# A mixture-of-experts stage on one core: router by pairwise maxima, half lists joined by a flip, the last shared block moved behind the experts

## The chip, the cores and the metric

The kernel runs on one core of a Trainium2 chip. Its time is the device time of one execution in microseconds (us), and a comparison uses the median of several runs. The engines are TensorE (PE; PEld is its weight load), VectorE (DVE), ScalarE (ACT), GpSimd (POOL) and SyncE (SP), which here only starts transfers. The transfers run on 16 DMA engines. Transfers that SyncE starts are on the hardware queue q1, those that GpSimd starts (gathers, scatter-adds, accumulating copies) on the software queue q0.

## What is computed

Four residual layers on x of 2048 tokens (4 x 512) and 512 features: an expert layer routed by token id, an MX-quantised feed-forward layer, cross attention, and last a mixture of 64 experts with a shared expert. Only the last is touched by the change:

```python
scores = sigmoid(x @ gate_w)                 # 2048 x 64
scores_b = scores + bias
gs = scores_b.reshape(-1, 8, 8)              # 8 groups of 8 experts
group_scores = sum(top_k(gs, 2)[0], -1)      # the two largest of each group
keep the 4 best groups, then the 6 best experts among them
w = scores of the six / their sum * 2.5
for each expert: its first 96 tokens (CAP = 96)
    h = silu(x @ w_gate) * (x @ w_up);  y += w * (h @ w_down)      # F = 192
shared = (silu(x @ ws_gate) * (x @ ws_up)) @ ws_down               # F = 192
x = x + tanh(g_ffn[1]) * (y + shared)
```

## The kernel before

Everything is fp32 in this stage. P = 128, D = 512, T = 2048 tokens = 16 tiles (NT), GCH = 4 blocks of 512 tokens, F1 = 192 = 128 + 64 (FR = 64 is the remainder).

The stage is one block of code (from line 1320) in which each engine has its own list of instructions in a fixed order. Semaphores connect them: `need(engine, sem, n)` waits until sem has counted n, and `own.link(...)` makes the next instruction of the same engine wait for this one.

- VectorE normalises the 16 tiles into xnb (line 1424). TensorE turns each (`turn_four`, 1551) through PSUM banks 0 and 1 in turn, and ScalarE copies the columns to XNT (1691). Two `logits` products (1561), each of two blocks, are copied out, turned back (1569) and put through Sigmoid (1700).
- `route(h)` on VectorE (1433 to 1481) treats tiles 0 to 7 (h = 0) and 8 to 15 (h = 1). It finds the two largest of each group by reductions and an equality mask (1438 to 1450), the four best groups by MAX8 and MATCH_REPLACE8 (1453, 1456), masks the others (1458 to 1465), finds the six best experts (1468, 1471), and writes a mask (1473), a key for each chosen token and expert (1476), and the weights selw (1477 to 1481).
- TensorE turns the keys (`turn_keys`, 1607), so that partition e + 64 h holds expert e's keys of token half h. ScalarE copies them (1731). VectorE's `largest` takes the 96 largest of 1024 keys, eight at a time: 12 MAX8 (1491), 11 MATCH_REPLACE8 (1493). TensorE moves the two half lists side by side (`turn_halves`, 1614), VectorE copies them (1498), takes the 96 largest of the 192, TensorE turns the result (`turn_lists`, 1619), and five VectorE instructions (1503 to 1508) make the row indices idx.
- The shared expert goes in four blocks of 512 tokens. `shared_up(g)` (364) does gate and up: a part of 128 features (m = 0) and a part of 64 (m = 1). ScalarE takes Silu and a copy (1716 to 1720), GpSimd multiplies (1366), `shared_down(g)` (1599) makes four tiles in banks 4 and 5, each by a product over 128 rows and one over 64. ScalarE scales and copies (1727), GpSimd adds into X (1370), and SyncE stores the tile to out (1333). TensorE's order is: up 0, up 1, down 0, keys, up 2, down 1, up 3, half lists, down 2, two tiles of down 3, lists, two tiles of down 3.
- SyncE loads the weights of the 32 expert pairs into 7 places (`load_pair`, 374 and 376). Pairs 0 and 1 are there long before. Pairs 2, 4 and 3 take the places of X tiles and of XNT when these have been read and stored.
- GpSimd gathers rows of 96 tokens per expert (1383). In the loop over pairs, TensorE turns rows (1639), multiplies gate and up (1648), turns the hidden (1656), and multiplies down (1667) as pairs of 64-row halves. VectorE copies the result (1528), and GpSimd scatter-adds it (1390): even experts into out, odd experts into odd_sum. At the end one accumulating transfer of 4 MB adds odd_sum to out (1413).

## Time and profile before

| | |
|---|---|
| runs, median (lowest to highest) | 1090.39 us (1089.48 to 1091.29), 3 runs |
| profiled execution: its time, its span | 1089.95 us, 1087.9 us |
| mean granted TensorE clock | 0.962 |
| busy: PE, DVE, POOL, ACT | 90%, 62%, 59%, 37% |

The span is the time from the first to the last instruction in the profile; 2.05 us lie around it. The busy share of TensorE is a mean over stages with different limits. In the part that the change touches, from about 640 us on, it is 1.00 through most of the expert loop and 0 in the last 28 us.

### The profile page before, as it was taken

The numbers are of one execution on the slowest core, as the hardware profiler recorded it, in microseconds if no ns is written. First come the engines' busy times: TensorE is split into PE (matmuls) and PEld (weight loads), VectorE is DVE, ScalarE is ACT, GpSimd is POOL, SyncE is SP. The second block draws the span as 40 slices with busy tenths as digits, with TensorE's granted clock in tenths as the row PEclk, the third lists the DMA queues.
The fourth block names the chain that finished last, engine by engine and source line by source line (L and its number), as shares of the span: only waits on it lengthen the run. The fifth ranks groups of instructions, "written<-read, shape, count | busy, mean of one in ns | idle before, by whom it ended". The sixth has DMA issues, their size and how long they took to land. (4 is left out here: it accounts for less than half of the span.)

```text
span 1087.9 us, 13655 instructions
## 1 busy us (share of the span) xinstructions
PE 975.8 (90%) x4400; PEld 473.8 (44%) x4400; DVE 673.8 (62%) x1244; ACT 400.9 (37%) x797; POOL 643.6 (59%) x564
## 2 busy tenths in 40 slices
PE   5989999479999998999999988997999999999960
PEld 4445544234444443444444443333555555555520
DVE  6689988968888887677777758891222222222220
ACT  4345444334444444666666633322111111111100
POOL 4487885668787887776776721345355555454530
PEclk9989999789999999999999999998999999999995
DMA  7664454420000001501006040148999999999547
GB/s 262 229 146 113 131 134 99 103 82 1 1 1 1 1 2 39 193 20 30 20 20 237 1 154 1 58 162 283 349 340 343 342 340 345 345 338 340 126 57 154
DMA packets 63124, 161.72 MB, mean 149 GB/s; under 512 B 9824, under 2 KB 9968, under 8 KB 62480
## 3 DMA queue, kind: packets, MB, share of 16 engines
q1 hardware_dynamic: 46880, 115.76, 30.2%
q0 software_dynamic: 16048, 40.91, 17.1%
q10 hardware_dynamic: 128, 4.19, 1.1%
q8 instruction: 37, 0.61, 0.2%
q14 instruction: 31, 0.25, 0.1%
HBM read 129.54 MB, written 39.67 MB: 156 GB/s over the span
## 5 line engine op out<-in xcount | busy, mean ns | idle before, releaser
L578 POOL TENSOR_TENSOR ARENA<-ARENA 128x512 f32<-128x512 f32 x128 | 133.2, 1062 | 54.2 <-DVE ARENA L821 54.2
L1390 POOL DMA_INDIRECT out<-ARENA,idx x32 | 46.2, 1445 | 131.7 <-DVE ARENA L1528 124.2
L1004 PE MATMUL PS<-SLAB,ARENA 128*128 128x512 bf16 x512 | 118.0, 382 | 6.7 <-DVE ARENA L772 4.6
L1755 ACT ACTIVATE ARENA<-PS 96x192 f32<-96x192 f32 x64 | 20.9, 326 | 227.5 <-PE PS L1648 227.5
L1528 DVE COPY ARENA<-PS 96x512 f32<-96x512 f32 x64 | 41.1, 682 | 93.9 <-PE PS L1667 93.9
L1225 ACT ACTIVATE ARENA<-PS,ARENA 128x512 f32<-128x512 f32 x128 | 86.8, 683 | 23.6 <-DVE ARENA L815 20.3
L815 DVE TENSOR_REDUCE ARENA<-PS 128x2 f32<-128x1024 f32 x64 | 78.2, 1222 | 6.9 <-PE PS L1038 6.5
L1648 PE MATMUL PS<-SLAB,ARENA 128*96 128x384 f32 x240 | 82.1, 495 | 0.0
L1004 PEld LDWEIGHTS PS<-SLAB,ARENA 128*128 128x128 bf16 x512 | 48.8, 98 | 67.8 <-issue 13.2
L1049 PEld LDWEIGHTS PS<-ident,ARENA 128*128 128x128 f32 x512 | 54.8, 141 | 51.1 <-issue 35.0
L1191 ACT ACTIVATE ARENA<-PS 128x512 f32<-128x512 f32 x64 | 38.2, 597 | 102.9 <-PE PS L1004 84.3
L534 POOL TENSOR_TENSOR ARENA<-ARENA 128x1024 bf16<-128x1024 fp8e4 x32 | 61.1, 1909 | 24.8 <-DVE ARENA L786 24.8
L528 POOL TENSOR_TENSOR ARENA<-ARENA 128x1024 f32<-128x1024 f32 x32 | 62.8, 1962 | 20.0 <-DVE ARENA L781 20.0
L958 PE MATMUL PS<-CT,XNT 128*128 x152 | 71.6, 615 | 2.2 <-ACT XNT L1129 2.1
L1038 PE MATMUL PS<-ARENA 64*128 64x512 f32 x256 | 73.2, 649 | 0.3 <-ACT ARENA L1225 0.2
L942 PE MATMUL PS<-CT,ARENA 128*128 x152 | 70.7, 609 | 2.9 <-ACT ARENA L1119 2.9
L1049 PE MATMUL PS<-ident,ARENA 128*128 128x128 f32 x512 | 70.7, 280 | 1.7 <-DVE XNT L828 1.7
L1516 DVE SCALAR_TENSOR_TENSOR ARENA<-PS,ARENA 96x192 f32<-96x192 f32 x64 | 26.2, 409 | 73.9 <-ACT ARENA L1755 73.9
L1383 POOL DMA_INDIRECT ARENA<-rows,idx x64 | 60.0, 937 | 19.7 <-issue 11.1
L1061 PE MATMUL PS<-XNT,CT 128*64 128x512 f32 x256 | 68.2, 616 | 0.0
L471 POOL TENSOR_TENSOR XNT<-XNT,ARENA 128x1536 f32<-128x1536 f32 x16 | 45.6, 2850 | 35.1 <-DVE ARENA L675 35.0
L1023 PE MATMUL PS<-SLAB,ARENA 128*128 128x512 bf16 x256 | 58.6, 380 | 0.0
(254 smaller groups left out, 1879.1 us busy)
## 6 DMA issues: line engine op xcount, KB each, us to landing
SLAB<-in_L_ffn_w_gate SPq DMA_DIRECT2D x30, 384.0 KB, 19.8
SLAB<-in_L_ffn_w_up SPq DMA_DIRECT2D x30, 384.0 KB, 20.8
X<-in_L_ffn_w_down SPq DMA_DIRECT2D x14, 768.0 KB, 18.5
SLAB<-in_L_ffn_w_down SPq DMA_DIRECT2D x10, 768.0 KB, 18.5
CT<-in_L_ffn_w_gate SPq DMA_DIRECT2D x16, 384.0 KB, 19.7
CT<-in_L_ffn_w_up SPq DMA_DIRECT2D x16, 384.0 KB, 21.0
X<-in_ctx SPq DMA_DIRECT2D x4, 1024.0 KB, 8.8
XNT<-in_L_ffn_w_gate SPq DMA_DIRECT2D x16, 256.0 KB, 2.6
```

The costliest lines, as they stand in the source:

```text
L528: pool.tensor_tensor(blocks(iy[:, h, :]), blocks(inter[:, par, h, :]), spread(iinv[:, h, :]), ALU.mult).then_inc(iy_ready, 1)
L534: pool.tensor_tensor(blocks(qi[:, par, h, :]), blocks(ic[:, h, :]), spread(im[:, par, h, :]), ALU.mult).then_inc(iq_ready, 1)
L578: last = pool.tensor_tensor(prob[s % 4][:, h, :], prob[s % 4][:, h, :], rec[:, s % 4, h:h + 1].to_broadcast([P, D]), ALU.mult)
L815: dve.tensor_reduce(nmax[:, s % 4, :], bank(2 * (s % 2), 2).rearrange("p (h d) -> p h d", h=2), AX.X, ALU.max, negate=True).then_inc(max_r ...
L942: last = pe.matmul(bank(2 + j % 2), hT[:, j % 2, k * P:(k + 1) * P], CT[:, bass.ds(e, 1), k, :].rearrange("p a s -> p (a s)"), start=(k == ...
L958: last = pe.matmul(bank(4 + j % 2), aT[:, j % 2, k * P:(k + 1) * P], CT[:, bass.ds(e, 1), k, :].rearrange("p a s -> p (a s)"), start=(k == ...
L1004: last = pe.matmul(bank(b), QT[:, par, k * P:(k + 1) * P], w[:, k, c * D:(c + 1) * D], start=(k == 0), stop=(k == KD - 1))
L1038: last = pe.matmul(bank(2 * (s % 2) + h), qn[rows_h, i % 2, c * P:(c + 1) * P], keys4[rows_h, i % 4, :], start=True, stop=True)
L1049: last = pe.transpose(bank(4 + h)[:, k * P:(k + 1) * P], prob[s % 4][:, h, k * P:(k + 1) * P], ident[:, :])
L1061: last = pe.matmul(bank(6 + i % 2)[h * DH:h * DH + DH, :], CT[:, b, k, r * P + h * DH:r * P + h * DH + DH], PT[h][i % 2][:, k, :], start=( ...
L1225: last = act.activation(prob[s % 4][:, h, :], bank(2 * (s % 2) + h), ACT.Exp, bias=nmax[:, s % 4, h:h + 1], accum_out=esum[:, s % 4, h:h + 1])
L1648: last = pe.matmul(bank(2 + e % 2)[0:CAP, 0:2 * F1].rearrange("p (n f) -> p n f", n=2), bT[:, e % 2, k, :], gate_up_of(e)[:, :, k, :], sta ...
```

## The change

Six things change, and nothing outside this stage.

1. The two largest of each group are found by pairwise `max` and `min` over neighbours: 64 columns to 32, 16 and 8 per tile, 10 two-input operations in place of three reductions, two masks and five narrow steps. Masking the groups is one operation that adds -1e30. The mask and the key product are one operation. The weights of both halves follow both passes.
2. ScalarE runs one Sigmoid on a dummy value ahead of the stage. Tiles are turned through four banks (0, 1, 4, 5), and a third group of four is turned ahead of the first logits.
3. The half lists are sorted, with zeros behind the last token. The second one is turned around by a product with a flip matrix and fills the empty end of the first, so the search over 192 and the last turn go.
4. The shared expert's down product takes two tiles at a time: the two products over 128 rows, then the remainders of 64 rows, one on partitions 0 to 63 and one on 64 to 127. ScalarE writes the remainders of every second tile to the other partitions, in four half copies.
5. TensorE's order is: up (0,0), (0,1), (1,1), keys, up (1,0), down 0, up 2, down 1, half lists, two tiles of down 2, flip, two tiles of down 2.
6. Block 3 of the shared expert moves behind the expert loop. Its raw X tiles 12 to 15 are stored to out early. Its products run after the last expert, and four accumulating transfers of 128 rows add them to out. The merge is split: rows of tiles 12 to 15 (1 MB) first, then the other 3 MB. The four transfers are issued once the first part has landed, on the same queue.

The diff, cut to its core:

```diff
+        NS = NT - KD
+        ORDER = [(0, 1), (1, 0), (0, 1), (0, 1)]
+
+        def up_count(g, m):
+
+            return 2 * g + ORDER[g].index(m) + 1
+
+        TURN = (0, 1, 4, 5)
+
+        def rest_of(a):
+
+            return a[:, D:SW].rearrange("p (q c) -> p q c", q=2)
+
+        def tiles_of(a, odd):
+
+            return a.rearrange("p (q two c) -> p q two c", q=2, two=2)[:, :, odd, :]
...
+                for i in range(NS, NT):
+                    sp.dma_start(out_v[:, i, :], X[:, i, :]).then_inc(acc_stored[2], 16)
...
                         sp.wait_ge(acc_stored[0], 64)
                         load_pair(sp, 2)
                     if i == 8:
-                        sp.wait_ge(sgu_done, 2 * GCH)
+                        sp.wait_ge(sgu_done, 2 * (GCH - 1))
                         load_pair(sp, 4)
-                    if i == 12:
+                    if i == NS - 1:
...
+                own.link(pool.memset(flip, 0.0))
+                pool.affine_select(out=flip, in_=flip, compare_op=ALU.not_equal, fill=1.0, base=1 - CAP,
+                                   pattern=[[1, CAP]], channel_multiplier=1).then_inc(iota2_set, 1)
...
-                pool.dma_start(out[0:T, :], odd_sum[0:T, :], accum_op=ALU.add, max_dma_last_dim=4 * 4 * D).then_inc(merged, 16)
+                pool.dma_start(out[NS * P:T, :], odd_sum[NS * P:T, :], accum_op=ALU.add, max_dma_last_dim=4 * 4 * D).then_inc(merged_l, 16)
+                pool.dma_start(out[0:NS * P, :], odd_sum[0:NS * P, :], accum_op=ALU.add, max_dma_last_dim=4 * 4 * D).then_inc(merged, 16)
+                pool.wait_ge(merged_l, 16)
+                for n in range(KD):
+                    pool.wait_ge(sh_ready, NS + n + 1)
+                    pool.dma_start(out_v[:, NS + n, :], sh_l[:, n, :], accum_op=ALU.add).then_inc(shared_added, 16)
...
+                    one_of, other = halves(sc_b[:, tiles].rearrange("p i e -> p (i e)"))
+                    dve.tensor_tensor(high, one_of, other, ALU.max)
+                    own.link(dve.tensor_tensor(low, one_of, other, ALU.min))
+                    dve.tensor_tensor(first4, *halves(high), ALU.max)
+                    dve.tensor_tensor(less4, *halves(high), ALU.min)
+                    own.link(dve.tensor_tensor(next4, *halves(low), ALU.max))
+                    own.link(dve.tensor_tensor(next4, next4, less4, ALU.max))
+                    dve.tensor_tensor(first8, *halves(first4), ALU.max)
+                    dve.tensor_tensor(less8, *halves(first4), ALU.min)
+                    own.link(dve.tensor_tensor(next8, *halves(next4), ALU.max))
+                    own.link(dve.tensor_tensor(next8, next8, less8, ALU.max))
...
+                    own.link(dve.tensor_scalar(gsm[:, 4, tiles], gext[:, tiles, 0:GROUPS], -BIG / 2, -BIG, ALU.is_gt, ALU.mult))
+                    own.link(dve.tensor_tensor(grouped(ext[:, tiles, 0:E1]), grouped(sc_b[:, tiles]),
+                                               gsm[:, 4, tiles].unsqueeze(3).to_broadcast([P, count, GROUPS, PERG]), ALU.add))
...
+                    dve.scalar_tensor_tensor(out=keyt[:, h], in0=ext[:, tiles, 0:E1], scalar=-1.5 * BIG, in1=spread(keyc[:, tiles], E1),
+                                             op0=ALU.is_le, op1=ALU.mult).then_inc(key_ready, 1)
+
+                def weights(h):
+
+                    tiles = slice(NT // 2 * h, NT // 2 * (h + 1))
+                    own.link(dve.scalar_tensor_tensor(out=selw[:, tiles], in0=ext[:, tiles, 0:E1], scalar=-1.5 * BIG, in1=scores_sb[:, tiles],
+                                                      op0=ALU.is_le, op1=ALU.mult))
...
                 route(0)
                 route(1)
+                weights(0)
+                weights(1)
...
+                for n in range(CAP // 8):
+                    eight = half_lists[:, 8 * n:8 * n + 8]
+                    if n == CAP // 8 - 1:
+                        dve.max(eight, keys).then_inc(list_ready, 1)
+                    else:
+                        own.link(dve.max(eight, keys))
+                        own.link(dve.match_replace(keys, eight, keys, 0.0))
+
                 dve.wait_ge(list_turned, 1)
+                dve.tensor_copy(both, bank(7)[0:CAP, 0:2 * E1].rearrange("p (h e) -> p h e", h=2)).then_inc(list_ready, 1)
+                dve.wait_ge(list_ready, 2)
                 dve.wait_ge(list_turned, 2)
+                own.link(dve.scalar_tensor_tensor(out=list_c, in0=both[:, 0, :], scalar=0.0, in1=bank(7)[0:CAP, 2 * E1:3 * E1],
+                                                  op0=ALU.is_equal, op1=ALU.mult))
+                own.link(dve.tensor_tensor(list_c, list_c, both[:, 0, :], ALU.add))
+                dve.tensor_scalar(emp[:, 0, :], list_c, 0.0, None, ALU.is_equal)
+                own.link(dve.tensor_scalar(emp[:, 1, :], list_c, -1.0, float(T), ALU.mult, ALU.add))
+                own.link(dve.scalar_tensor_tensor(out=emp[:, 0, :], in0=emp[:, 0, :], scalar=rowf[0:CAP, 0:1],
+                                                  in1=emp[:, 1, :], op0=ALU.mult, op1=ALU.add))
+                dve.tensor_copy(idx[0:CAP, :], emp[:, 0, :]).then_inc(idx_ready, 1)
...
+                dve.wait_ge(ssil_ready, up_count(GCH - 1, 0))
+                dve.tensor_tensor(hs_l[:, 0:D], ssil_l[:, 0:D], bank(1), ALU.mult).then_inc(hs_ready, 1)
+                dve.wait_ge(ssil_ready, up_count(GCH - 1, 1))
+                dve.wait_ge(ub_ready, 2 * GCH - 1)
+                dve.tensor_tensor(hs_l[:, D:SW], ssil_l[:, D:SW], ub_l, ALU.mult).then_inc(hs_ready, 1)
...
+                def shared_down(g, two, into, product):
+
                     pe.wait_ge(hs_ready, 2 * g + 2)
+                    for n in range(2):
+                        pe.matmul(bank(into[n]), product[:, (2 * two + n) * P:(2 * two + n + 1) * P], wsd[:, 0, :], start=True, stop=False)
+                    for n in range(2):
+                        rows_n = slice(n * FR, (n + 1) * FR)
+                        pe.matmul(bank(into[n]), rest_of(product)[rows_n, two, :], wsd[rows_n, 1, :],
+                                  start=False, stop=True).then_inc(sd_done, 1)
+
+                def shared_two(g, two):
+                    need(pe, sh_ready, 4 * g + 2 * two - 2)
+                    if g == 0:
+                        pe.wait_ge(key_out, 2)
+                    shared_down(g, two, ((4, 5), (2, 3))[two], hs[g % 2])
...
+                    pe.transpose(bank(7)[0:CAP, 0:2 * E1], half_lists, ident[:, :]).then_inc(list_turned, 1)
+
+                def turn_around():
                     pe.wait_ge(list_ready, 2)
+                    pe.matmul(bank(7)[0:CAP, 2 * E1:3 * E1], flip[0:CAP, :], both[:, 1, :], start=True, stop=True).then_inc(list_turned, 1)
+
+                pe.wait_ge(sw_in, 80)
+                shared_up(0, 0)
+                shared_up(0, 1)
+                shared_up(1, 1)
                 turn_keys()
+                shared_up(1, 0)
+                for two in range(2):
+                    shared_two(0, two)
+                shared_up(2, 0)
+                shared_up(2, 1)
+                for two in range(2):
+                    shared_two(1, two)
                 turn_halves()
+                shared_two(2, 0)
+                pe.wait_ge(iota2_set, 2)
+                turn_around()
+                shared_two(2, 1)
...
+                pe.wait_ge(bt_out, E1)
+                shared_up(GCH - 1, 0)
+                pe.wait_ge(ht6_out, PAIRS)
+                shared_up(GCH - 1, 1)
+                pe.wait_ge(h6_ready, E1)
+                shared_down(GCH - 1, 0, (2, 3), hs_l)
+                pe.wait_ge(o_ready, E1)
+                shared_down(GCH - 1, 1, (4, 5), hs_l)
...
+                act.activation(rsum[:, 0:1], neg_half[:, 0:1], ACT.Sigmoid)
...
                 columns_out(1)
+                columns_out(2)
                 logits_out(0)
-                columns_out(2)
+                columns_out(3)
                 scores_out(0)
-                columns_out(3)
                 logits_out(1)
                 scores_out(1)
...
+                        for odd in range(2):
+                            last = act.activation(rest_of(ssil)[odd * FR:(odd + 1) * FR], tiles_of(bank(6)[0:FR, :], odd), ACT.Silu)
+                        last.then_inc(ssil_ready, 1)
+                        for odd in range(2):
+                            last = act.activation(rest_of(ub)[odd * FR:(odd + 1) * FR], tiles_of(bank(6)[FR:2 * FR, :], odd), ACT.Copy)
+                        last.then_inc(ub_ready, 1)
...
+                shared_hidden(0, 0)
+                shared_hidden(0, 1)
+                shared_hidden(1, 1)
                 for r in range(4):
                     act.wait_ge(xn_stored[r], XN0 + 16 * NT // 8)
                 keys_out(0)
                 keys_out(1)
+                shared_hidden(1, 0)
+                shared_out(0)
+                shared_hidden(2, 0)
+                shared_hidden(2, 1)
                 shared_out(1)
...
+                act.wait_ge(h6_ready, E1)
+                act.wait_ge(sgu_done, up_count(GCH - 1, 0))
+                act.activation(ssil_l[:, 0:D], bank(0), ACT.Silu).then_inc(ssil_ready, 1)
+                act.wait_ge(sgu_done, up_count(GCH - 1, 1))
+                for odd in range(2):
+                    last = act.activation(rest_of(ssil_l)[odd * FR:(odd + 1) * FR], tiles_of(bank(6)[0:FR, :], odd), ACT.Silu)
+                last.then_inc(ssil_ready, 1)
+                for odd in range(2):
+                    last = act.activation(ub_l.rearrange("p (q c) -> p q c", q=2)[odd * FR:(odd + 1) * FR],
+                                          tiles_of(bank(6)[FR:2 * FR, :], odd), ACT.Copy)
+                last.then_inc(ub_ready, 1)
+                for n in range(KD):
+                    act.wait_ge(sd_done, NS + n + 1)
+                    act.activation(sh_l[:, n, :], bank((2, 3, 4, 5)[n]), ACT.Copy, scale=tgate[:, 3:4]).then_inc(sh_ready, 1)
```

## Rows read from the trace of the kernel before

**Rows 1.** Chain that ended last: start us, length us, engine, output, line, instructions.

```profile
664.74 21.10 PE PS L364 x64
685.84 8.43 PE PS L1599 x16
...
696.10 1.24 DVE CT L1491
697.36 1.30 DVE ARENA L1493 x2
...
726.41 12.65 PE PS L1599 x24
...
741.77 1.10 POOL ARENA L1383
...
743.17 7.37 DMA ARENA<-rows,idx
...
751.50 3.65 PE PS L1648 x8
...
755.60 2.58 PE PS L1648 x8
...
765.06 2.75 PE PS L1667 x12
...
774.41 2.75 PE PS L1667 x12
...
1055.94 4.12 DMA odd_sum<-ARENA,idx
```

**Rows 2.** Waits of SyncE's queue, 740:1060 us: total us, times, longest us.

```profile
SPq L376 <- PE PS L1667: 68.9, 25, 6.1
```

**Rows 3.** Timeline of the tail: start us, us, engine, line, operation [idle before].

```profile
1052.68 1.29 DVE L1528 COPY ARENA<-PS 96x512 f32<-96x512 f32 x2 [2.92 <-PE PS L1667]
...
1061.94 1.13 POOL L1413 DMA_DIRECT2D out<-odd_sum  x1 [4.59 <-issue]
```

**Rows 4.** DMA view, 1030:1090: issues, KB each, median us to landing.

```profile
out<-odd_sum POOLq DMA_DIRECT2D x1, 4096.0 KB, 22.9
```

**Rows 5.** DMA view, 1070:1080: packets, MB, share of 16 engines.

```profile
q0 software_dynamic: 256, 2.10, 100.6%
```

**Rows 6.** Timeline of the first route pass, ScalarE and VectorE, 652:674.

```profile
653.74 1.28 ACT L1700 ACT_TABLE_LOAD   x1
...
655.73 0.69 DVE L1433 TENSOR_TENSOR CT<-ARENA 128x512 f32<-128x512 f32 x1 [8.11 <-ACT ARENA L1700]
...
661.53 0.22 DVE L1450 TENSOR_TENSOR ARENA<-ARENA 128x64 f32<-128x64 f32 x1
...
663.75 0.20 DVE L1458 TENSOR_SCALAR ARENA<-ARENA 128x64 f32<-128x64 f32 x1
...
666.15 0.07 DVE L1465 MEMSET ARENA<- 128x16 f32 x1
...
669.12 0.43 DVE L1473 TENSOR_SCALAR CT<-ARENA 128x512 f32<-128x512 f32 x1
...
670.19 0.69 DVE L1477 TENSOR_TENSOR CT<-CT,ARENA 128x512 f32<-128x512 f32 x1
...
671.65 0.60 ACT L1716 ACTIVATE ARENA<-PS 128x512 f32<-128x512 f32 x1 [4.97 <-PE PS L364]
...
672.14 0.69 DVE L1481 TENSOR_TENSOR CT<-CT,ARENA 128x512 f32<-128x512 f32 x1
```

**Rows 7.** Timeline of the second route pass, GpSimd beside VectorE.

```profile
687.24 1.80 POOL L1366 TENSOR_TENSOR CT<-ARENA 64x512 f32<-64x512 f32 x1 [2.38 <-ACT ARENA L1720]
687.84 2.98 DVE L1477 TENSOR_TENSOR CT<-CT,ARENA 128x512 f32<-128x512 f32 x1
```

**Rows 8.** Windows view, 740:760: busy us by engine, granted clock, DMA share, GB/s.

```profile
740.00:760.00 20.00, 13.46 (x44) 7.01 (x44) 2.22 (x4) 3.99 (x8) 11.16 (x11) 0.83 0.83 289
```

**Rows 9.** DMA view, 1050:1060: packets, MB, share of 16 engines.

```profile
q0 software_dynamic: 448, 0.79, 62.9%
```

More of the change, by code:

```diff
@@ L1425, in _, with halves, grouped @@
                                       ALU.subtract, ALU.mult).then_inc(xn_ready, 1)
+                dve.memset(gext, BIG)
+                own.link(dve.memset(ext[:, :, E1:SEC], BIG))
+                dve.wait_ge(iota2_set, 2)
+                own.link(dve.tensor_scalar(rowf[0:CAP], rowf[0:CAP], -float(T), None, ALU.add))
                 dve.wait_ge(bias_in, 32)
+                def halves(a):
+                    v = a.rearrange("p (n two) -> p n two", two=2)
+                    return v[:, :, 0], v[:, :, 1]
+                def grouped(a):
+                    return a.rearrange("p i (g n) -> p i g n", n=PERG)
                 def route(h):
@@ L1431, in route @@
                     tiles = slice(first, first + count)
+                    half = count * E1
+                    most = tmp[:, tiles].rearrange("p i e -> p (i e)")
+                    high, low = most[:, 0:half // 2], most[:, half // 2:half]
+                    room = selw[:, tiles].rearrange("p i e -> p (i e)")
+                    first4, less4, next4 = (room[:, n * half // 4:(n + 1) * half // 4] for n in range(3))
+                    first8, less8, next8 = (gsm[:, n, tiles].rearrange("p i g -> p (i g)") for n in range(3))
```

189 lines of the change are left out of this document (61 added, 128 removed).

## The prediction

> **What bounds the kernel now.** I read the chain of waits first, because the share of busy time (TensorE 90%) mixes stages with different limits. Up to 694.9 us the router stage is TensorE's: two blocks of shared up products (21.10) and one of down products (8.43) run without a gap before the keys are turned [rows 1]. Then VectorE holds the chain: twelve searches (MAX8, then MATCH_REPLACE8) over 1024 keys, 1.24 + 1.30 each, from 696.10 until TensorE takes over half a microsecond before 726.41 [rows 1]. TensorE turns the half lists, and the next link is 12.65 us of shared down products: they hide VectorE's second search (12 searches over 192) and end at 726.41 + 12.65 = 739.06, when the last turn can run [rows 1]. The first gather is issued at 741.77, the second needs 7.37 to land [rows 1].
>
> From there the expert loop is pure TensorE with a period of 774.41 - 765.06 = 9.35 us per pair of experts [rows 1]. It isn't held by weights: SyncE's queue waits 68.9 us in total for slots to come free, so loads are asked for as soon as there is room [rows 2]. Whatever moves the first gather therefore moves the whole loop. After the last expert's result (copied from 1052.68 [rows 3]) come its scatter-add (1055.94, 4.12 to land [rows 1]) and the 4 MB merge, issued at 1061.94 [rows 3] and landed 22.9 later, near 1085 [rows 4]. In the merge the software queue keeps all 16 DMA engines full (100.6%), with 256 packets in 10 us [rows 5]. The tail is bound by DMA engines, and TensorE is idle in it.
>
> **Scores and the two route passes.** The Sigmoid table load (1.28) stands right in front of the first scores, which start VectorE at 655.73 [rows 6]. A dummy activation moves it ahead of the stage, and a third group of four tiles is turned before the logits, through four banks. ScalarE has four more copies ahead of the scores than before, but they follow the transposes closely. I take 1.6 earlier: VectorE starts at 654.1. Bounds 0.5 and 2.5.
>
> One pass lasts from 655.73 to 670.2, where the weights begin: 14.5 [rows 6]. Three parts shrink.
> - Top two of each group: reductions, masks and a memset from 656.4 (655.73 + 0.69) to 661.75, 5.3 [rows 6]. The new block has 2 operations with 256 results, 4 with 128, and 5 with 64. Rows give 0.22 for width 64 and 0.69 for 512 [rows 6], so 0.42 and 0.29 between. By results written that is 2 x 0.42 + 4 x 0.29 + 5 x 0.22 = 3.1, with gaps 3.45. But 8 of the 11 read every second word, and no row shows such a read. As the upper bound I price them by the width walked: 2 x 0.69 + 3 x 0.42 + 3 x 0.29 + 0.29 + 2 x 0.22 = 4.25, with gaps 4.6. I take the upper one, so 0.7 is saved (the other end saves 1.85).
> - Masking groups and filling ext: from 663.75 to the end of a memset at 666.22, 2.5 [rows 6], becomes one narrow and one wide operation with gaps, 0.95: 1.55 saved.
> - Mask (0.43) and key product (0.69 by its width) become one operation: 0.45 saved [rows 6].
>
> So a pass costs 14.5 - 2.7 = 11.8, two passes 23.6. The Trainium skill, "Vector Engine (DVE) Microarchitecture Reference", section 5.2, says that a port keeps its full rate only for runs of two or more adjacent words, and lists 1.7 to 2.5 ns a column where a step breaks them. By it the pairwise operations would come out near my upper bound. No row of this case tests it.
>
> **GpSimd beside VectorE.** The 0.69 product of line 1477 took 2.98 in the second pass, while GpSimd ran a product of 1.80 and went on with an add [rows 7]. Three GpSimd products (one of 512 columns, two of 256) now fall into the second pass and the weights. I charge 2.0, between 0 and 4. The Trainium skill, "GPSIMD Engine Reference", section 8, has the two engines share their SBUF interfaces when VectorE has two SBUF inputs, which fits that row.
>
> **Weights moved behind both passes.** From 670.19 to 672.83 is 2.64 per half [rows 6], 5.3 for both. They now hide the turning and copying of the keys, which took 1.8 (696.10 less the end of the down products, 685.84 + 8.43 [rows 1]), so they replace that wait and add 3.5. The search over 1024 starts at 654.1 + 23.6 + 2.0 + 5.3 = 685.0 rather than 696.10: 11.1 gained.
>
> Will TensorE be there? Even if it starts the shared products as late as now (664.74), it needs for (0,0) 6.9 (671.65 - 664.74 [rows 1, 6]), for its remainder 3.6, a wait of some 1.6 for ScalarE's four half copies, and for (1,1) 3.6: 680.4. The keys come at 679.7, and the weights cover 5.3 behind that. Moving the table load and the logits forward adds several microseconds of room.
>
> **Joining the lists.** The twelve rounds keep their 29.7 and end at 714.7. In between TensorE has 6.9 + 10.5 of up products and 4 two-tile down products. Two tiles cost four full instructions (0.53 each, 8.43/16 [rows 1]) or less, and four on row halves at 0.23 (2.75/12 [rows 1], the loop's own 64-row pairs): 3.0. It is done near 710 and waits some 5 us. The second search, with its 23 steps and the copy of 192 columns goes; what is left is
>
> 0.3 (one transpose) + 4.6 (two down tiles, queued on TensorE ahead of the flip product; VectorE waits for them) + 0.3 (flip) + 1.6 (seven small VectorE steps) + 1.2 (the first gather stands behind adds of tiles 8 and 9 on GpSimd, and VectorE's two-input steps can meet these adds) = 8.0.
>
> The 4.6 is 3.0 plus 1.5 because TensorE comes out of an idle stretch. After the 4 us wait for the second gather the same eight matmuls took 3.65 and then 2.58 [rows 1], and the granted clock of that stretch is 0.83 [rows 8], so part of it ran at 1.2 GHz. The first gather is issued at 714.7 + 8.0 = 722.7 rather than 741.77: 19.1 gained in all, bounds 14 and 24.
>
> **What keeps its place.** SyncE's queue now sends pair 4's weights at the time of the first gather, and pair 3's behind tile 11's store. Before, pair 3's load lay beside the second gather, and that row's 7.37 already contains such company. The chain from the first gather to the second row keeps its 8.8. Pair 3 lands near 742 and is read at about 758. Raw tiles 12 to 15 are stored early, in a free stretch. The loop's waits on shared results end before the gather lands. Cost 0.
>
> **The tail.** The shared block's up and down products (10.5 + 6, ScalarE and VectorE steps near 3) start at 1052.7 in old time and end near 1073, under the merge (until about 1085). They cost nothing while the merge lasts. But four accumulating transfers of 128 rows of 2 KB are added on the same software queue, and they start behind its 3 MB. Four scatter-adds of 96 rows kept the engines at 62.9% of 10 us [rows 9]: 16 x 6.29/384 = 0.26 engine-us per row with its index reads. 512 rows on 16 engines are 8.4, without index reads some 7.5 (my estimate). By bytes alone (256 packets of 8 KB in 10 us, so 1 MB in 5) it is 5.0. With completion of each showing once it could be 9. I take 7.5, since the row size matches.
>
> **Sum.** 1089.95 (profiled execution, span 1087.9) - 19.1 + 7.5 = 1078.4. The median, 1090.39, lies 0.4 above the profiled one, so as a median 1078.8.
>
> **Rivals.**
> - *Lean head:* pairwise steps cost by results written (2.3 less), GpSimd never meets VectorE (2 less), the clock stays up: 24 gained. 1090.4 - 24 + 7.5 = 1073.9. For it: searches of one input ran at 1.24 all along beside GpSimd's adds [rows 1]. Chance 0.17.
> - *Tail hidden:* the shared tiles slip into gaps of the merge and cost 1: 1072.3. Against it: engines at 100.6% [rows 5]. Chance 0.12.
> - *Fat head:* GpSimd's blocking doubles, TensorE's slow clock lasts through the last down pair, gathers land 2 later beside pair 4: 14 gained, 1083.9. Chance 0.14.
> - *Row halves run one after the other:* the change would not do what it says. Two times 0.46 more ahead of the flip product, hidden elsewhere: 1079.7. Against it: the loop's 64-row pairs at 0.23. Chance 0.02.
> - *The tail takes back more than the head gives:* the four transfers go one at a time after the merge, each with issue (1.4) and landing (4.12 [rows 1]), 5.5 each, 22 in all: 1090.4 - 19.1 + 22 = 1093.3, slower. It decides from 4.8 per tile on. Against it: GpSimd issues them as soon as 1 MB has landed, without waiting between them. Chance 0.05.
>
> **Chances.** The forecast itself has 0.50. A measurement of this kernel can tell about 0.2%, 2.2 us, from no change. All cases but the slow one lie far below; 0.02 of the fat head may end within 2.2. So faster 0.93, same 0.02, slower 0.05. The range from 1072 to 1085 takes in the forecast with its bounds, the fat head, nearly all of the lean head and half of the hidden tail; about 0.15 is left out.
>
> **What would show it.** In the profile after: MAX8 over 1024 starting near 685 (right: 682 to 688), pairwise operations of 256 results at 0.4 or 0.7, the first indirect gather near 723, the loop's period unchanged at 9.35, TensorE idle for some 5 us before the half lists are turned, the merge ending some 19 earlier and followed by 5 to 9 us of 2 KB packets. I am wrong if the loop waits for weights, if TensorE and not VectorE releases the search, or if the last packets cost over 10 us.

## The result and the profile after

| | kernel before | changed kernel |
|---|---|---|
| median (lowest to highest) | 1089.93 us (1088.33 to 1091.29) | 1076.81 us (1074.62 to 1077.39) |
| ratio, 95% interval | | 0.9881 (0.9865 to 0.9896) |
| span of the profiled execution | 1087.9 us | 1075.6 us |

The changed kernel is 1.2% faster, 13.1 us by the medians. The forecast was 1078.8, range 1072 to 1085. The ratios in this document leave out one execution, of e7_odd_rows_loaded, which took 1640.33 us at a granted clock of 0.56.

The chain of waits of the changed kernel shows where VectorE now starts its search over 1024 keys, and what stands between the end of that search and the first gather (start us, length us, engine, output, line):

```profile
656.27 0.42 DVE CT L1486
656.69 0.35 DVE CT L1487
...
667.82 1.39 DVE CT L1491
...
681.34 0.69 DVE CT L1525
682.03 1.15 DVE CT L1538
...
710.37 1.24 DVE CT L1536
...
711.65 0.41 PE PS L1666
712.06 3.34 PE PS L1644 x4
715.39 1.06 PE PS L1647 x4
716.45 0.33 PE PS L1670 x2
...
717.38 1.18 DVE CT L1548
...
718.70 1.18 DVE CT L1550
...
720.39 1.10 POOL ARENA L1411
...
721.79 9.23 DMA ARENA<-rows,idx
...
731.98 4.46 PE PS L1707 x8
...
736.88 2.58 PE PS L1707 x8
...
746.35 2.75 PE PS L1726 x12
...
755.70 2.75 PE PS L1726 x12
```

Against [rows 1]: the link of two up blocks and one down block ahead of the keys is gone, the pieces from 656 to 682 are VectorE's own passes and weights without a wait, the search has the same steps of 1.24 and 1.30, and the 12.65 us link behind it has become 0.41 + 3.34 + 1.06 + 0.33. The first gather is issued at 720.39 rather than 741.77. The row that starts the loop needs 9.23 to land rather than 7.37, and the first product takes 4.46 rather than 3.65. The loop's period is unchanged: 755.70 - 746.35 = 9.35.

The tail, from the timeline (start us, us, engine, line, operation [idle before]):

```profile
1034.68 1.28 DVE L1571 COPY ARENA<-PS 96x512 f32<-96x512 f32 x2 [2.92 <-PE PS L1726]
...
1043.87 0.94 POOL L1441 DMA_DIRECT2D out<-odd_sum  x1 [4.61 <-issue]
1044.47 1.35 POOL L1442 DMA_DIRECT2D out<-odd_sum  x1
...
1052.15 1.75 POOL L1446 DMA_DIRECT2D out<-ARENA  x2 [6.34 <-ACT ARENA L1858]
...
1054.56 1.72 POOL L1446 DMA_DIRECT2D out<-ARENA  x2 [0.66 <-ACT ARENA L1858]
```

and its DMA view, 1050:1060 us (packets, MB, share of 16 engines; issues, KB each, median us to landing):

```profile
q0 software_dynamic: 283, 2.19, 105.2%
out<-ARENA POOLq DMA_DIRECT2D x4, 256.0 KB, 16.6
```

The last result is copied from 1034.68, 18.0 earlier than in [rows 3], and the span ends 12.3 earlier: the tail behind that copy grew from 35.2 to 40.9 us. The last shared block is ready just in time: GpSimd waits for ScalarE's results and issues the four transfers at 1052.15 and 1054.56. They land 16.6 us after their issue, on engines as full as in [rows 5].

**How the profiles are compared from here on.** The part ahead of the stage is the same work in every kernel, but for the one dummy Sigmoid, yet the stage's first VectorE instruction starts at 638.61 in the profile of before, at 641.09 in that of the changed kernel, and between 636.8 and 643.2 in all fourteen profiles. So every time below is counted from that instruction. "Search" is the start of the first MAX8 over 1024, "gather" the issue of the first gather, "loop" the time from there to the copy of the last result, "tail" the time from there to the end of the span. Each is the difference of starts in a timeline.

| kernel | ratio to before (95%) | search | gather | loop | tail | end |
|---|---|---|---|---|---|---|
| before | | 57.5 | 103.2 | 310.9 | 35.2 | 449.3 |
| changed | 0.9881 (0.9865 to 0.9896) | 40.9 | 79.3 | 314.3 | 40.9 | 434.5 |
| e0_after_again | 0.989 (0.9866 to 0.9913) | 40.8 | 79.5 | 313.1 | 41.2 | 433.7 |
| e1_no_shared_adds | 0.9843 (0.9813 to 0.9873) | 40.9 | 79.5 | 313.1 | 35.2 | 427.8 |
| e2_before_new_passes | 1.0004 (0.9989 to 1.0019) | 54.9 | 100.5 | | | 446.6 |
| e3_flip_first | 0.9878 (0.9843 to 0.9913) | 40.8 | 79.8 | 313.9 | 41.3 | 434.9 |
| e4_flip_first_adds_late | 0.9857 (0.983 to 0.9885) | 41.6 | 74.4 | 316.7 | 41.2 | 432.2 |
| e5_pair4_late | 0.9858 (0.9816 to 0.9899) | 40.9 | 73.8 | 315.3 | 41.0 | 430.0 |
| e6_one_transfer | 0.9877 (0.985 to 0.9904) | 40.9 | 79.9 | 313.1 | 40.9 | 434.0 |
| e7_odd_rows_loaded | 0.9793 (0.974 to 0.9845) | 41.7 | 80.3 | 313.5 | 35.9 | 429.7 |
| e9_remainders_apart | 0.9849 (0.9804 to 0.9894) | 40.9 | 78.5 | 312.9 | 41.1 | 432.4 |
| e10_keys_behind_down0 | 0.9964 (0.9941 to 0.9988) | 51.2 | 90.1 | 313.8 | 41.3 | 445.1 |
| e11_best | 0.9721 (0.9697 to 0.9744) | 41.6 | 74.4 | 310.1 | 36.3 | 420.7 |
| e12_busy_wait | 0.986 (0.9832 to 0.9888) | 41.6 | 78.4 | 312.4 | 41.3 | 432.1 |

The ratios of the single edits have intervals of 0.3 to 1.0%, which is as much as most edits are worth. The columns of the stage repeat within about 1 us, as the changed kernel, run again unedited, shows:

> The changed kernel again, unedited, so that the edits of this group are compared with it on the same chip. Theory: a ratio of 0.988 to the kernel before, as first measured, and stage times relative to the stage's first instruction (first gather 79.3 us, end 434.5 us behind it) that repeat within 1 us, while the part ahead of the stage moves by some 2 us from one execution to the next. Rival (part of the first result came from ahead of the stage): the stage's own times differ by over 2 us.

The ratio comes back within 0.001, the gather within 0.2 us, the end within 0.8 us and the loop within 1.2 us. The theory holds.

### The profile page after: what moved, and what is told of

Its sections match the earlier page's. It is cut to its first block and busy times, and to the rows that moved or that the text cites. A ratio compares the mean times of both kernels' runs of the same rounds, so it can differ in the third digit from the quotient of the medians.

```text
span 1075.6 us, 13598 instructions
## 1 busy us (share of the span) xinstructions
PE 962.3 (89%) x4376; PEld 471.0 (44%) x4398; DVE 657.7 (61%) x1204; ACT 400.4 (37%) x805; POOL 639.4 (59%) x565
## 5 line engine op out<-in xcount | busy, mean ns | idle before, releaser
L579 POOL TENSOR_TENSOR ARENA<-ARENA 128x512 f32<-128x512 f32 x128 | 133.4, 1063 | 54.2 <-DVE ARENA L822 54.1
L1005 PE MATMUL PS<-SLAB,ARENA 128*128 128x512 bf16 x497 | 116.5, 382 | 8.3 <-DVE ARENA L773 5.1
L1571 DVE COPY ARENA<-PS 96x512 f32<-96x512 f32 x64 | 41.1, 681 | 94.6 <-PE PS L1726 94.6
L1192 ACT ACTIVATE ARENA<-PS 128x512 f32<-128x512 f32 x64 | 38.2, 597 | 103.2 <-PE PS L1005 84.6
L1411 POOL DMA_INDIRECT ARENA<-rows,idx x64 | 60.2, 940 | 19.6 <-issue 11.1
L1024 PE MATMUL PS<-SLAB,ARENA 128*128 128x512 bf16 x249 | 57.9, 380 | 0.6 <-issue 0.3
```

What stands on the lines that cost most here:

```text
L579: last = pool.tensor_tensor(prob[s % 4][:, h, :], prob[s % 4][:, h, :], rec[:, s % 4, h:h + 1].to_broadcast([P, D]), ALU.mult)
L1005: last = pe.matmul(bank(b), QT[:, par, k * P:(k + 1) * P], w[:, k, c * D:(c + 1) * D], start=(k == 0), stop=(k == KD - 1))
```

## The experiments

### What the new passes are worth by themselves

The kernel before with only VectorE's passes replaced:

```diff
-                    own.link(dve.tensor_reduce(g1, by_group, AX.X, ALU.max))
-                    own.link(dve.tensor_tensor(tmp_group, by_group, spread(g1, PERG), ALU.is_equal))
...
+                    dve.tensor_tensor(high, one_of, other, ALU.max)
+                    own.link(dve.tensor_tensor(low, one_of, other, ALU.min))
...
                 route(0)
                 route(1)
+                weights(0)
+                weights(1)
```

> The kernel before, with only VectorE's two route passes and the weights as in the changed kernel (pairwise maxima, one masking operation, one key operation, weights behind both passes); TensorE's order, the two searches and the shared blocks stay. Theory (TensorE's products hold the keys up to 694.9 us in the kernel before, so faster passes alone free only VectorE): keys are ready some 9 us earlier, the search over 1024 starts where it did, and the time is that of before within 1.5 us. Rival (the passes were on the path): 8 to 9 us less, near 1081.

Measured: ratio 1.0004 (0.9989 to 1.0019), no difference. The first MAX8 over 1024 in its timeline:

```profile
692.74 1.23 DVE L1502 MAX8 CT<-ARENA 128x8 f32<-128x1024 f32 x1 [12.47 <-ACT ARENA L1742]
```

VectorE waits 12.47 us in front of it. What lets it in is ScalarE's copy of the turned keys, which stands behind TensorE's down products of block 0, as in the kernel before. Every microsecond of the faster passes goes into that wait. (The search starts 2.6 us sooner than in the profile of before. That isn't the passes': the second logits product took 3.65 here and 5.25 there, and the granted clock of the stretch from 638 to 664 was 1.00 here and 0.87 there, so part of it ran at the lower of the two levels. TensorE's instructions up to there are the same in both. So at least 1.6 of the gain that the profile of before suggests looks like a chance of that one execution, which fits the 13.1 of the medians against the 14.8 of the profiles.)

### What the place of the keys is worth

The changed kernel with the turn of the keys back behind block 0's down products (and, in parts cut here, behind ScalarE's copies of them):

```diff
...
                 shared_up(1, 1)
-                turn_keys()
                 shared_up(1, 0)
                 for two in range(2):
                     shared_two(0, two)
+                turn_keys()
...
```

> The changed kernel with only the turn of the keys put back behind up (1,0) and the two down pairs of block 0 on TensorE, and behind their copies on ScalarE. Theory (the passes are worth something only because TensorE turns the keys early; in the kernel before its products held them): the keys leave TensorE near 689 us instead of 677 and the search over 1024 starts 8 to 9.5 us later; TensorE's wait ahead of the half lists grows by as much, nothing is given back, and the time is 1085 to 1086. Rival (the keys' place matters little, the removed second search carries the gain): 1 to 3 us more.

Measured: ratio 0.9964 (0.9941 to 0.9988), search 10.4 us later, end 10.6 later. The theory holds, a little stronger than expected. Nothing is given back behind it. With e2 this says how the gain ahead of the first gather is made. The passes alone give nothing, and without the early keys the changed kernel loses some 11 of its 14.8 us. The early keys with the old passes weren't run. By the lengths of the passes (14.5 and 15.1 in the profile of before, 10.0 and 11.3 in that of the changed kernel) the search would then start some 8 us later, so most of the 11 us need both; this part is an estimate.

### The price of the last shared block in the tail

The transfers left out:

```diff
                 for n in range(KD):
                     pool.wait_ge(sh_ready, NS + n + 1)
-                    pool.dma_start(out_v[:, NS + n, :], sh_l[:, n, :], accum_op=ALU.add).then_inc(shared_added, 16)
...
```

> The changed kernel without the four accumulating transfers of the last shared block: it leaves out the shared expert's part of rows 1536 to 2047. TensorE, ScalarE and VectorE still do that block's products after the expert loop. Theory (the tail is bound by the DMA engines, which process the four transfers behind the 3 MB of the merge): the time falls by what 512 rows of 2 KB cost, 5 to 7.5 us, from 1076.8 to about 1071, and the span ends some 2.5 us after the last 8 KB packet, as before the change. Rival (the block's products or the completion of four semaphores end the kernel, not the packets): the time falls by 1.5 us at most.

Measured: ratio 0.9843 (0.9813 to 0.9873), tail 35.2, which is the tail of before to a tenth. The 5.7 us are those transfers', all of them, and the block's products under the merge cost nothing. The theory holds. The time fell to 1070.55 us, within what was expected.

I had priced them by rows of 2 KB. One transfer of the same 1 MB in packets of 8 KB:

```diff
-                for n in range(KD):
-                    pool.wait_ge(sh_ready, NS + n + 1)
-                    pool.dma_start(out_v[:, NS + n, :], sh_l[:, n, :], accum_op=ALU.add).then_inc(shared_added, 16)
+                pool.wait_ge(sh_ready, NT)
+                pool.dma_start(out[NS * P:T, :].rearrange("(p n) d -> p (n d)", n=KD), sh_l.rearrange("p n d -> p (n d)"),
+                               accum_op=ALU.add).then_inc(shared_added, 16)
...
```

> The changed kernel with the last shared block added by one accumulating transfer of 128 packets of 8 KB instead of four of 128 packets of 2 KB (the block's tokens are dealt to the tiles so that a partition holds four consecutive rows). The merge stays in two parts. Theory (packets of 2 KB cost more per byte than packets of 8 KB on the DMA engines): the part behind the merge shortens from 6 to 5 us, some 1 us less than the changed kernel. Rival (e7's gain of some 5 us came from the packet size and the single transfer, not from reading odd_sum plainly): 3 to 5 us less.

Measured: ratio 0.9877 (0.985 to 0.9904), tail 40.9. Both expectations fall: a quarter of the packets, and the time is the same within 0.1 us. The DMA views from 1063 to 1075 us, first of the changed kernel, then of this one:

```profile
q0 software_dynamic: 663, 1.63, 74.4%
```

```profile
q0 software_dynamic: 224, 1.57, 67.4%
```

663 packets or 224 move about the same 1.6 MB in the last stretch. Between these two packet sizes an accumulating transfer costs by its bytes, near 5.7 us per MB, and not by its packets.

So the way to a shorter tail is to accumulate less. SyncE loads the last 1 MB of odd_sum plainly, and VectorE adds it on the way out of PSUM:

```diff
-                pool.dma_start(out[NS * P:T, :], odd_sum[NS * P:T, :], accum_op=ALU.add, max_dma_last_dim=4 * 4 * D).then_inc(merged_l, 16)
...
+                sp.wait_ge(added[1], 16 * PAIRS)
+                sp.dma_start(odd_l.rearrange("p n d -> p (n d)"),
+                             odd_sum[NS * P:T, :].rearrange("(p n) d -> p (n d)", n=KD)).then_inc(merged_l, 16)
...
+                    dve.scalar_tensor_tensor(out=sh_l[:, n, :], in0=bank((2, 3, 4, 5)[n]), scalar=tgate[:, 3:4], in1=odd_l[:, n, :],
+                                             op0=ALU.mult, op1=ALU.add).then_inc(sh_ready, 1)
```

> The changed kernel with another end: SyncE loads the last 1 MB of odd_sum into SBUF, VectorE adds it to the last shared block straight from PSUM, and one accumulating transfer of 128 packets of 8 KB adds the sum to out; the merge keeps only its 3 MB, and the tokens of the block are dealt to the tiles so that a partition holds four consecutive rows. Theory (the tail is the DMA engines' work: 4 MB of merge at 5 us each and 6 us of 2 KB packets now; 3 MB of merge, 1 MB accumulated in 8 KB packets, and a plain load of 1 MB that costs about 3 us in the edited kernel): 2.5 to 3 us less, near 1074. Rival (the sum waits for the load, TensorE and VectorE, so the last transfer starts late): no change or slower.

Measured: ratio 0.9793 (0.974 to 0.9845), tail 35.9, which is 5.0 less where 2.5 to 3 was expected. The load costs at most 0.7 us, by which this tail is longer than that of before. Its issue and GpSimd's, from the timeline, and the landing from the DMA view (KB, us to landing):

```profile
1039.85 0.33 SPq L1382 DMA_DIRECT2D CT<-odd_sum  x1
...
1041.71 1.07 POOL L1449 DMA_DIRECT2D out<-odd_sum  x1 [4.67 <-issue]
...
CT<-odd_sum SPq DMA_DIRECT2D x1, 1024.0 KB, 4.7
```

SyncE starts 1.9 us ahead of GpSimd's own issue, so most of the 4.7 us to landing fall ahead of the merge. The total of accumulated bytes is 4 MB as in the kernel before, and the tail is the same but for the 0.7.

### What stands between the search and the first gather

The flip product ahead of the two down tiles:

```diff
+                pe.wait_ge(iota2_set, 2)
+                turn_around()
                 shared_two(2, 0)
-                pe.wait_ge(iota2_set, 2)
-                turn_around()
```

> The changed kernel with the flip product ahead of the first two down tiles of block 2, instead of behind them. Theory (two things end the wait for the first gather: the flip product queued behind 4.4 us of down products, and GpSimd's adds of tiles 8 and 9 that stand ahead of the gather): the indices are ready some 4 us earlier, but the adds come some 1 us later than now, so the first gather moves by less than 1 us and the time stays at 1076.8 within 1.5 us. Rival (the flip product's place alone decides): 3.5 to 4 us less, near 1073.

Measured: ratio 0.9878 (0.9843 to 0.9913), gather 79.8 against 79.3, no gain. The last VectorE step and the first gather:

```profile
711.42 0.19 DVE L1552 CAST idx<-CT 96x64 int32<-96x64 f32 x1
...
717.93 1.10 POOL L1411 DMA_INDIRECT ARENA<-rows,idx  x1 [0.17 <-issue]
```

The indices lie ready for over 6 us while GpSimd is busy with adds that wait for the down tiles. The theory holds. Moving the adds as well:

```diff
-                into_x(NS - 4)
-                into_x(NS - 3)
                 pool.wait_ge(idx_ready, 1)
...
                 gather(1)
+                into_x(NS - 4)
+                into_x(NS - 3)
```

> The edit of e3_flip_first and GpSimd's adds of tiles 8 and 9 behind the first two gathers. Theory: VectorE's steps to the indices no longer meet an add (1.9 us less), the first gather is issued 5 to 6 us earlier and lands before pair 4's weights are asked for; the third gather moves by only 1 to 2 us and lands beside these weights, so TensorE waits for it: some 4 us less in all, near 1072.5. Rival (the wait only moves to the third gather): 1 us less or nothing.

Measured: ratio 0.9857 (0.983 to 0.9885), gather 4.9 earlier than in the changed kernel, loop 2.4 longer, end 2.3 earlier (1.5 earlier than in e0). TensorE does wait for the third gather, as the theory said, but the gain lies between the theory's 4 us and the rival's 1. TensorE's row for the third expert:

```profile
728.12 0.92 PE L1696 MATMUL PS<-ident,ARENA 96*128 96x96 f32 x4 [4.24 <-DMA ARENA<-rows,idx]
```

Next, gathers 2 and 3 ahead of the last two adds, and pair 4's weights asked for only behind gather 3:

```diff
                         sp.wait_ge(sgu_done, 2 * (GCH - 1))
+                        sp.wait_ge(g_in6[3], 16)
                         load_pair(sp, 4)
...
                 into_x(NS - 3)
+                gather(2)
+                gather(3)
                 into_x(NS - 2)
                 into_x(NS - 1)
...
```

> The edits of e4_flip_first_adds_late, gathers 2 and 3 ahead of the adds of tiles 10 and 11, and SyncE asks for pair 4's weights only when gather 3 has landed. Theory (in e4 the third gather, issued 20 us before it was needed by nobody else, landed after 7.9 us beside these weights and TensorE waited 4.2 us): the third gather lands within 4 to 5 us, TensorE does not wait for it, and the kernel is 4 us shorter than e4, near 1069. Rival (the loads only come late elsewhere: pairs 4 and 3 or 5 are then missing in the loop): as e4 or slower.

Measured: ratio 0.9858 (0.9816 to 0.9899), end 2.2 earlier than e4 instead of 4; the ratios of the two are the same. The wait for the third gather is gone: its product follows at once, and the first eight matmuls run at full speed. But a new wait ends 29 us later:

```profile
719.04 2.82 PE L1710 MATMUL PS<-SLAB,ARENA 128*96 128x384 f32 x8 [0.60 <-issue]
...
737.09 0.34 SPq L374 DMA_DIRECT2D X<-in_L_ffn_w_gate  x1
...
748.49 6.99 PE L1710 MATMUL PS<-X,ARENA 128*96 128x384 f32 x16 [4.61 <-issue]
```

Both theory and rival hold in part. The tile X in the last row is pair 3's place: its weights were asked for at 737.09, because their load waits for stores that stood behind pair 4's load on the same queue, and TensorE stands still for 4.61 us. The view names nothing that ends this wait; that it is the weights is read from their late issue, and from e11 below, where they are asked for earlier and the wait is gone.

### Row halves, and TensorE's clock behind a wait

Each remainder directly behind its tile:

```diff
                     for n in range(2):
                         pe.matmul(bank(into[n]), product[:, (2 * two + n) * P:(2 * two + n + 1) * P], wsd[:, 0, :], start=True, stop=False)
-                    for n in range(2):
                         rows_n = slice(n * FR, (n + 1) * FR)
```

> The changed kernel with each tile's 64-row product directly behind its 128-row product, so that the two 64-row products no longer follow one another. Theory (two products on different row halves run at the same time, and only one pair of tiles stands on the path): a pair of tiles takes some 1 to 1.5 us more on TensorE, the first gather comes 1 to 1.5 us later, the rest lies beside the search and the merge, and the time is 1077 to 1079. Rival (no overlap of row halves in this form): the same duration of a pair and the same time.

The same pair of tiles, first in the changed kernel, then apart:

```profile
687.65 1.98 PE L1644 MATMUL PS<-ARENA 128*128 128x512 f32 x4
...
689.57 1.13 PE L1647 MATMUL PS<-ARENA 64*128 64x512 f32 x4
```

```profile
684.89 1.12 PE L1644 MATMUL PS<-ARENA 128*128 128x512 f32 x2
685.95 1.12 PE L1646 MATMUL PS<-ARENA 64*128 64x512 f32 x2
687.00 1.12 PE L1644 MATMUL PS<-ARENA 128*128 128x512 f32 x2
688.06 1.12 PE L1646 MATMUL PS<-ARENA 64*128 64x512 f32 x2
```

Row halves do overlap, and they save their time: from 684.89 to 689.11 is 4.2 us apart, from 687.65 to 690.62 is 3.0 together. Yet the gather comes 0.8 us earlier apart, not 1 to 1.5 later, and the ratio is 0.9849 (0.9804 to 0.9894). The expectation on the gather fails. Windows rows around the pair that stands ahead of the flip product, changed kernel first (stretch, its length, busy us of PE, PEld, DVE, ACT and POOL, granted clock, DMA share, GB/s):

```profile
707.00:712.00 5.00, 0.64 (x4) 0.35 (x3) 4.49 (x5) 1.27 (x2) 3.09 (x3) 0.97 0.53 200
712.00:718.00 6.00, 6.00 (x15) 2.04 (x14) 1.34 (x4) 1.27 (x2) 0.75 (x1) 0.74 1.02 334
```

```profile
700.00:708.00 8.00, 8.00 (x16) 2.12 (x15) 7.42 (x8) 3.45 (x7) 4.31 (x4) 1.00 0.17 66
708.00:714.00 6.00, 6.00 (x15) 2.00 (x15) 1.27 (x4) 2.06 (x3) 3.42 (x4) 1.00 0.59 192
```

In the changed kernel TensorE is done early, stands still for 4.36 us, and then runs part of the pair at 1.2 GHz (granted clock 0.74). Apart, it is busy until the half lists come and keeps 2.4 GHz. What the faster form saves in the queue it loses behind the wait: the flip product starts 34.4 us behind the start of the search in the changed kernel (716.38) and 34.5 apart (712.46).

The 0.8 us of the gather come from another place. One of VectorE's narrow steps behind the flip product stands beside an add of GpSimd in the changed kernel, and falls between two adds in this one, since the adds come one tile at a time:

```profile
718.70 1.17 DVE L1550 SCALAR_TENSOR_TENSOR CT<-CT,ARENA 96x64 f32<-96x64 f32 x1
```

```profile
714.78 0.28 DVE L1550 SCALAR_TENSOR_TENSOR CT<-CT,ARENA 96x64 f32<-96x64 f32 x1
```

Back to the clock. Five products into an unused bank, in place of the wait, test just that:

```diff
+                for n in range(5):
+                    pe.matmul(bank(7), ident[:, :], wsd[:, 0, :], start=True, stop=True)
                 turn_halves()
```

> The changed kernel with five more 128x512 products on TensorE into an unused bank ahead of the turn of the half lists, in place of its 4.4 us of waiting. Theory (the two down tiles ahead of the flip product take 4.4 us instead of 3.0 because TensorE comes out of its wait at the lower granted clock): the pair takes 3.0, the granted clock of that stretch is 1.00 instead of 0.74, and the first gather comes 1 to 1.4 us earlier relative to the stage. Rival (the four instructions are slow for another reason, transfers of pair 2's weights beside them): the pair stays at 4.4.

```profile
713.30 1.91 PE L1644 MATMUL PS<-ARENA 128*128 128x512 f32 x4
715.13 1.13 PE L1647 MATMUL PS<-ARENA 64*128 64x512 f32 x4
```

```profile
709.00:715.00 6.00, 6.00 (x15) 2.27 (x14) 4.28 (x6) 1.07 (x2) 2.59 (x3) 1.00 0.65 219
```

The pair takes 2.9 us up to the flip product, where by the same rows it took 4.5 in the changed kernel, at a granted clock of 1.00 and with pair 2's weights in flight as before. The gather comes 0.9 earlier, although the search itself began 0.7 later: counted from the search, 36.8 rather than 38.4. The theory holds and the rival falls. Ratio 0.986 (0.9832 to 0.9888).

### Everything together

e4's order on GpSimd and TensorE, e5's gathers, e7's end, and the loads in the order in which they are needed:

```diff
-                    if i == 8:
-                        sp.wait_ge(sgu_done, 2 * (GCH - 1))
-                        load_pair(sp, 4)
                     if i == NS - 1:
                         sp.wait_ge(acc_stored[1], 128)
+                        sp.wait_ge(g_in6[3], 16)
                         load_pair(sp, 3)
+                        sp.wait_ge(sgu_done, 2 * (GCH - 1))
+                        load_pair(sp, 4)
```

> The flip product first, adds of tiles 8 to 11 behind gathers 0 and 1 and around gathers 2 and 3, pair 3's weights and then pair 4's asked for behind tile 11's store and gather 3, and the end of e7. Theory (in e5 the head gained 8.4 us and the loop lost 4.6 because pair 3's load stood behind pair 4's and the stores that it waits for; with pair 3 first nothing is missing in the loop): the head gains 7 to 8 us and the end 5 us against the changed kernel, a ratio of 0.976 to 0.977 to the kernel before, near 1064. Rival (the weights are late again, pair 4 or 5): the loop waits 3 us or more and the ratio is 0.980.

Measured: 1059.37 us median (1058.64 to 1061.53), ratio 0.9721 (0.9697 to 0.9744), faster than expected (0.976 to 0.977). Pair 3 is now asked for 12 us earlier than in e5, counted from the stage's first instruction, and TensorE's products follow one another without the gap of e5, those with pair 3's weights (tile X) too:

```profile
726.61 0.34 SPq L374 DMA_DIRECT2D X<-in_L_ffn_w_gate  x1
...
728.54 5.33 PE L1721 MATMUL PS<-SLAB,ARENA 128*96 128x384 f32 x16
...
737.82 5.40 PE L1721 MATMUL PS<-SLAB,ARENA 128*96 128x384 f32 x16
...
747.17 5.40 PE L1721 MATMUL PS<-X,ARENA 128*96 128x384 f32 x16
```

Against the changed kernel its gather is 4.9 earlier, its loop 4.2 shorter and its tail 4.6 shorter: 13.8 counted from the stage's first instruction. The change under study is worth 14.8, so this makes it nearly twice as much.

## Why the prediction was right, and where its terms were off

The direction, the range and most of the mechanism held. Several terms were off. That the sum still came out within 1.5 us of the medians (11.6 to 13.1) is partly luck: the steps ahead of the first gather gained 4.8 more than predicted, and the loop took 2 to 3 of that back. "Measured" is counted from the stage's first instruction.

| step | predicted | measured |
|---|---|---|
| start of the first pass | 1.6 earlier | 2.7 earlier (17.1 to 14.5) |
| pairwise block of a pass | 4.6 (upper bound), from 5.3 | 2.9 (656.27 to 659.13) |
| one pass | 11.8 | 10.0 and 11.3 |
| GpSimd beside VectorE | 2.0 | 1.3 |
| weights | 5.3 | 5.1 |
| start of the search | 11.1 earlier | 16.6 earlier |
| end of the search to the gather | 8.0 | 8.8 |
| first gather | 19.1 earlier | 23.9 earlier |
| from the gather to the last result | 0 | 3.4 longer, 2.2 in the second profile |
| tail | 7.5 longer | 5.7 longer |
| sum | 11.6 | 14.8 (profiles), 13.1 (medians) |

- **Who holds what.** That TensorE held the keys until 694.9 is confirmed by e2 (faster passes alone change nothing) and by e10 (late keys cost 10.6). The argument on TensorE's room (ready at 680.4 at the latest, with weights to cover it) held with several microseconds to spare: the search starts without a wait at 682.03.
- **The pairwise block** is the largest wrong term. I took the upper bound, by the width walked, and let section 5.2 of the Trainium skill's "Vector Engine (DVE) Microarchitecture Reference" support it. The rows say 0.42 for 256 results and 0.29 for 128, exactly what the line through 0.22 and 0.69 of [rows 6] gives for results written. The page's penalty for words that aren't adjacent doesn't show for a step of two. The operations without a link even overlap with their neighbours (0.35 in the chain for a duration of 0.42), so the block beat my lower bound of 3.45 too. This is the first of the three conditions of *lean head*. The gain up to the gather, 23.9, is that rival's 24 and the end of my bounds, although its other two conditions failed: GpSimd did meet VectorE, and the clock did fall. Some 1.6 of the 23.9 belong to the profile of before.
- **GpSimd beside VectorE.** In the second pass one operation of 0.29 takes 1.38; it begins 0.05 us after GpSimd's product of 1.27. Two more are held up where I had put only 1.2 us of a queue: the narrow steps at 717.38 and 718.70 take 1.18 each, beside the adds of tiles 8 and 9, and the first of them has a single tensor as input. These steps and the adds end almost together, the adds at 719.8 and the indices at 720.1, so without the delays of VectorE the adds would have held the gather almost as long. e3 shows that (79.8 with the indices early), and with the flip product first and the adds behind the gathers it comes at 74.4 (e4).
- **TensorE's clock behind the wait** was priced right (4.6, measured 4.4), and e12 shows it to be the clock.
- **"What keeps its place: cost 0"** failed. Pair 4's weights beside the first gathers are worse company than pair 3's beside the second alone: the second row lands 9.23 rather than 7.37 after its issue, and TensorE starts the loop after a longer wait at the lower clock. I had named 2 us of it under *fat head* and left it out of the sum. e11 shows that it was avoidable: with the loads asked for later and in another order its loop takes 310.1, against 314.3.
- **The tail.** The mechanism was right: the four transfers' own bytes behind a full queue, and not the block's products (e1). Its size was taken from rows of 2 KB as scatter-adds move them, 7.5, where the bytes alone gave 5.0. e6 shows that the bytes decide; the lower end of the range was the nearer one. Why the busy time per row of scatter-adds was no measure for these transfers isn't shown; scatter-adds also read indices and come one or two at a time.
- **Sum.** The part up to the first gather gained 4.8 more than predicted, the loop took back 2 to 3, the tail took 1.8 less. By the profiles the stage gains 14.8 us; by spans only 12.3, since the part ahead of it happened to be 2.5 us longer.

## What to carry to other kernels

When two engines are late in turn (VectorE's passes, TensorE's queue ahead of the keys), shortening one of them can gain nothing, as e2 shows, and an edit must be judged with its partner. Work moved under a transfer is free only until its own result needs the same DMA engines: count the bytes that are accumulated, and replace an accumulation by a plain load where an engine can add. Faster stages make transfers start together, so ask which of the loads is needed first, and put the issue order of each queue in that order.

## What the runs showed of the hardware that I hadn't expected

- VectorE reads every second fp32 word from SBUF at the full rate: a two-input operation with 256 results took 0.42 us, with 128 results 0.29, which is the line through contiguous ones (0.22 for 64, 0.69 for 512).
- An accumulating transfer to memory costs by bytes: 1 MB in 512 packets of 2 KB or in 128 of 8 KB left the same tail (40.9 us), 5.7 us more than without it.
- A faster form can be worth nothing through the clock. TensorE waited 4.4 us and ran the next 6 us at a mean granted clock of 0.74. With two remainders side by side on row halves, which saves 1.2 us per pair of tiles, the pair behind the wait ended no earlier than with the slower form that kept TensorE busy at 1.00.
- A narrow VectorE step can cost six times its length beside GpSimd: the same 96x64 step took 0.19 in e4 and 1.18 beside an add in the changed kernel.
- The same work ahead of the stage took from 636.8 to 643.2 us in fourteen profiled executions. I didn't find out why.
